# Router logits with the router's weights as the stationary operand, turned once per sequence

## What is computed

```
logits = x.astype(jnp.float32) @ gate_w.astype(jnp.float32).T        # (512, 256) @ (256, 8) for each sequence
scores = jax.nn.softmax(logits, axis=-1)
topk_w, topk_i = jax.lax.top_k(scores, K)                            # K = 2
topk_w = topk_w / (topk_w.sum(-1, keepdims=True) + 1e-20) * SCALE
...
return y + _swiglu_mlp(identity, sw_gate, sw_up, sw_down)            # the experts' sum, and the shared expert
```

## Time and profile before

| | |
|---|---|
| device time, median of 3 runs | 2029.63 us (2025.75 to 2030.84) |
| span of the profiled execution, first to last instruction | 1935.2 us |
| time around the span (median less span) | 94.4 us |
| TensorE busy / granted clock, mean | 1745.9 us (90%) / 0.959 |
| VectorE, ScalarE, GpSimd busy | 65%, 52%, 41% |

### The profile page before, as it was taken

The page is one execution under the profiler, slowest core; times in us unless marked ns, Lnnn a source line. Parts: engine busy times, 40 slices in busy tenths (PEclk is TensorE's granted clock), DMA queues, the critical chain, the costliest instruction groups (busy, mean ns, idle before and its releaser), DMA issues.

```text
span 1935.2 us, 41720 instructions
## 1 busy us (share of the span) xinstructions
PE 1745.9 (90%) x12978; PEld 1428.4 (74%) x12979; DVE 1265.4 (65%) x3121; ACT 997.8 (52%) x2314; POOL 792.4 (41%) x970
## 2 busy tenths in 40 slices
PE   0699999999999999988899995999999999999995
PEld 0466666666666666655788894999999999978884
DVE  3477788888888787876667766533333333367885
ACT  0366676767767666666433333444444444434553
POOL 2045555555555555555368774000000000067771
PEclk9889899999999888998799998999999999999997
DMA  2555556666555564562264533222222222247884
GB/s 46 87 83 84 100 90 109 111 111 107 104 105 104 101 107 90 95 115 91 67 204 162 172 129 127 63 73 73 73 73 71 72 73 73 76 153 184 223 203 75
DMA packets 175902, 205.94 MB, mean 106 GB/s; under 512 B 28209, under 2 KB 142450, under 8 KB 175762
## 3 DMA queue, kind: packets, MB, share of 16 engines
q1 hardware_dynamic: 153874, 161.66, 37.9%
q0 software_dynamic: 20736, 41.96, 8.3%
q10 hardware_dynamic: 1152, 0.52, 0.2%
HBM read 84.34 MB, written 68.81 MB: 79 GB/s over the span
## 4 chain that ended last, share of the span: by engine, by line
PE 70%; DVE 8%; ACT 6%; issue 5%; POOL 5%; DMA 2%; SPq 2%; ACTq 1%; POOLq 0%; DVEq 0%
PE bank L2295 5%; PE bank L1530 5%; PE bank L485 5%; PE bank L2296 4%; PE bank L487 4%; PE bank L2297 4%; PE bank L486 4%; PE bank L1585 4%; PE bank L1550 4%; PE bank L1532 3%; PE bank L1531 3%; ACT prob L1026 3%; PE bank L2316 3%; PE bank L2318 3%; PE bank L2317 3%
## 5 line engine op out<-in xcount | busy, mean ns | idle before, releaser
L2438 POOL DMA_INDIRECT f_y<-yg_scratch,index_all x128 | 129.8, 1014 | 552.8 <-DMA yg_scratch<-b_y 514.1
L897 POOL TENSOR_SCALAR_AFFINE_SELECT prob<-prob 128x512 f32<-128x512 f32 x256 | 163.4, 638 | 397.4 <-ACT prob L1026 397.3
L1026 ACT ACTIVATE prob<-bank 128x512 f32<-128x512 f32 (+1 forms) x512 | 249.1, 539 | 117.2 <-PE bank L1572 114.6
L2186 DVE TENSOR_TENSOR b_h<-b_h,bank 128x352 f32<-128x352 f32 x136 | 70.9, 521 | 291.7 <-ACT b_h L2134 291.7
L1305 DVE COPY_PREDICATED bank<-from_prev,bank 128x512 f32<-128x512 int32 x192 | 133.0, 693 | 107.5 <-PE bank L1550 103.7
L1308 DVE TENSOR_REDUCE row_max<-bank 128x4 f32<-128x512 f32 x256 | 177.3, 693 | 27.7 <-PE bank L1550 20.4
L2295 PE MATMUL bank<-wgu_h,bxT_h 128*128 x544 | 180.5, 332 | 0.7 <-DVE bxT_l L2181 0.3
L2296 PE MATMUL bank<-wgu_l,bxT_h 128*128 x544 | 176.9, 325 | 0.0
L2297 PE MATMUL bank<-wgu_h,bxT_l 128*128 x544 | 176.1, 324 | 0.0
L2134 ACT ACTIVATE b_h<-bank 128x352 f32<-128x352 f32 x136 | 63.2, 465 | 211.4 <-PE bank L2297 211.3
L1585 PE MATMUL bank<-prob,v_sb 128*32 128x256 f32 (+1 forms) x2048 | 164.1, 377 | 0.5 <-ACT pvT L1033 0.5
(11 more groups left out here) (338 smaller groups left out, 5104.0 us busy)
## 6 DMA issues: line engine op xcount, KB each, us to landing
bx<-xg_scratch SPq DMA_DIRECT2D x136, 128.0 KB, 2.1
yg_scratch<-b_y SPq DMA_DIRECT2D x136, 128.0 KB, 1.7
kS<-qk_h SPq DMA_DIRECT2D x128, 128.0 KB, 3.7
qS<-qk_h SPq DMA_DIRECT2D x128, 128.0 KB, 5.9
x_in<-in_L_attn_x_dram SPq DMA_DIRECT2D x16, 512.0 KB, 4.9
kS<-qk_l SPq DMA_DIRECT2D x64, 128.0 KB, 4.9
qS<-qk_l SPq DMA_DIRECT2D x64, 128.0 KB, 6.7
x_res<-in_L_attn_x_dram SPq DMA_DIRECT2D x16, 512.0 KB, 3.9
```

The source lines that it names most:

```text
L897: op = e.affine_select(out=own, in_=own, compare_op=ALU.is_gt, fill=0.0, base=0, pattern=[[0, HG], [1, P]], channel_multiplier=-1)
L1026: e.activation(prob[:, u % SLOTS, 2 * hp:2 * hp + 2, 0:w], src[:, :, 0:w], ACT.Exp, scale=SCALE).then_inc(keyed.frees[hp], 1)
```

## The change

`logits` swaps its operands: `wr`, padded with zeros to 32 columns, becomes the stationary operand, and the turned rows `rF` the moving one, 128 columns a matmul. The four row tiles go to four column tiles of the array (32 columns each) and to four groups of 32 partitions in PSUM. The logits then lie with experts along partitions. So ACT copies them to SBUF (`keep_logits`, into a piece of `wgu_l` that is not yet in use), TensorE turns the 128 x 128 block in one transposing matmul (`turn_logits`), and DVE reads that (`take_logits`). The turned block lies in `psum[3]`, a bank in which `gate_up` puts results for odd n; so `gate_up(M,1)` now waits for `lg_read`, the count of `take_logits` done. On DVE, `take_logits("b",M)` and `choose_first("b",M)` come after `hidden_low(m,5)`, and `take_logits("a",M)` right behind `choose_second("b",M)` rather than in the middle of step M. In step 0, `take_logits("a",0)` stays where it was and now waits for a turn on TensorE behind `gate_up(0,2)`.

```diff
...
         pos_f = sb("pos_f", [P, T, 2])
-        wr = sb("wr", [P, C, E])
+        wr = sb("wr", [P, (C - 1) * E + PAD])
         before = sb("before", [P, P])
...
         rF = arena[:, 2 * T * D:2 * T * D + C * S].rearrange("p (c s) -> p c s", c=C)
+        lg_kept = wgu_l[:, E * C - 1, 1, 0:P].bitcast(f32)
         items = {"a": rows_a, "b": rows_b}
...
             xh2_ready, copied_a = sem("xh2_ready"), sem("copied_a")
+            lg_turned, lg_read = sem("lg_turned"), sem("lg_read")
             pos_ready, member_ready = sem("pos_ready"), sem("member_ready")
...
                 reached(pe, *small.drained(m, name))
-                for t in range(T):
-                    for c in range(C):
-                        op = nc.tensor.matmul(small_bank(name, m)[:, t * E:(t + 1) * E], rF[:, c, t * P:(t + 1) * P], wr[:, c, :],
-                                      start=(c == 0), stop=(c == C - 1))
+                for c in range(C):
+                    for t in range(T):
+                        op = nc.tensor.matmul(small_bank(name, m)[t * PAD:(t + 1) * PAD, 0:P], wr[:, c * E:c * E + PAD],
+                                      rF[:, c, t * P:(t + 1) * P], start=(c == 0), stop=(c == C - 1), skip_group_check=True)
                 op.then_inc(small.full(name), 1)
+
+            def turned_bank(kind, m):
+
+                return SM[0][:, P:2 * P] if m == 0 else psum[3][:, 0:P] if kind == "b" else psum[3][:, P:2 * P]
+
+            def turn_logits(pe, kind, m):
+
+                if m >= HALF:
+                    return
+                pe.wait_ge(*small.read(m, f"lg{kind}"))
+                reached(pe, lg_read, item_of(kind, m))
+                nc.tensor.matmul(turned_bank(kind, m), lg_kept, ident[:, :],
+                                 start=True, stop=True, is_transpose=True).then_inc(lg_turned, 1)
+
+            def keep_logits(act, kind, m):
+
+                if m >= HALF:
+                    return
+                name = f"lg{kind}"
+                act.wait_ge(*small.filled(m, name))
+                reached(act, lg_turned, item_of(kind, m))
+                nc.scalar.activation(lg_kept, small_bank(name, m)[:, 0:P], ACT.Copy).then_inc(small.free(name), 1)
...
                     return
-                name = f"lg{kind}"
-                route.begin(item_of(kind, m))
-                dve.wait_ge(*small.filled(m, name))
-                nc.vector.tensor_copy(L, small_bank(name, m)[:, 0:T * E].rearrange("p (t x) -> p t x", t=T)).then_inc(small.free(name), 1)
+                dve.wait_ge(lg_turned, item_of(kind, m) + 1)
+                nc.vector.tensor_copy(L, turned_bank(kind, m).rearrange("p (t x) -> p t x", t=T)[:, :, 0:E]).then_inc(lg_read, 1)
...
                     return
-                dve.wait_ge(*small.read(m, f"lg{kind}"))
+                route.begin(item_of(kind, m))
+                dve.wait_ge(lg_read, item_of(kind, m) + 1)
                 largest(dve, L, m1, k1, oh1)
...
                 if n == 4:
+                    keep_logits(act, "b", m + 1)
                     rows_copy(act, "a", m + 1)
+                if n == FCS - 1:
+                    keep_logits(act, "a", m + 1)
...
                     sp.dma_start(full, src).then_inc(piece_in[0], 16)
+                sp.wait_ge(ffn_zeroed, 1)
                 with nc.allow_non_contiguous_dma(reason="the router's 2048 weights, once"):
                     for c in range(C):
-                        sp.dma_start(wr[:, c, :], gate_w[:, c * P:(c + 1) * P].rearrange("e p -> p e")).then_inc(router_in, 16)
+                        sp.dma_start(wr[:, c * E:(c + 1) * E], gate_w[:, c * P:(c + 1) * P].rearrange("e p -> p e")).then_inc(router_in, 16)
                 body(SEQS - 1, 1)
...
                     e.memset(before[:, :], 1.0).then_inc(ffn_zeroed, 1)
-                    pool_.wait_ge(ffn_zeroed, 1)
+                    pool_.wait_ge(ffn_zeroed, 2)
                     e.affine_select(out=before[:, :], in_=before[:, :], compare_op=ALU.is_gt, fill=0.0, base=0,
...
                             select(i, u)
+                        if at(i, SEQS - 1) and u == 0:
+                            e.memset(wr[:, :], 0.0).then_inc(ffn_zeroed, 1)
                         if u == 2 and live(before):
...
                             rows_copy(act, "b", 0)
+                            keep_logits(act, "b", 0)
                         if at(i, SEQS - 1) and 8 <= u < 8 + 2 * C:
...
                     first_chunk(act, 0, n)
+                    if n == 1:
+                        keep_logits(act, "a", 0)
                 normed(2, SEQS - 1, x_res, (0, 1))
...
                             turn_rows(pe, "a", 0)
+                            turn_logits(pe, "b", 0)
                         if u == 7 and live(nxt):
...
                         hi, lo = (w[:, k, :, :].rearrange("p k f -> p (k f)") for w in (wgu_h, wgu_l))
+                        if k == CHUNKS - 1:
+                            gp.wait_ge(lg_turned, 2 * HALF)
                         gp.wait_ge(stage_in, 32 * (k + 1))
...
                             place(dve, "b", m)
-                            take_logits(dve, "a", m)
                             hidden_low(dve, m, 1, h_f, h_h, h_l)
...
                         hidden(dve, m, 4, h_f)
-                        take_logits(dve, "b", m + 1)
                         hidden_low(dve, m, 4, h_f, h_h, h_l)
-                        choose_first(dve, "b", m + 1)
                         hidden(dve, m, 5, h_f)
...
                         hidden_low(dve, m, 5, h_f, h_h, h_l)
+                        take_logits(dve, "b", m + 1)
+                        choose_first(dve, "b", m + 1)
                         choose_second(dve, "b", m + 1)
+                        take_logits(dve, "a", m + 1)
                     expert_blocks()
...
                         if m > 0:
+                            pe.wait_ge(lg_read, 2 * m + 2)
                             gate_up(pe, m, 1, rT_h, rT_l)
...
                         gate_up(pe, m, 2, rT_h, rT_l)
+                        if m == 0:
+                            turn_logits(pe, "a", 0)
                         shared_down(pe, m, 0, h_h, h_l)
                         gate_up(pe, m, 3, rT_h, rT_l)
+                        if m == 0:
+                            pe.wait_ge(lg_read, 2)
                         turn_rows(pe, "b", m + 1)
...
                         gate_up(pe, m, 5, rT_h, rT_l)
+                        turn_logits(pe, "b", m + 1)
                         if m == HALF - 1:
...
                             gate_up(pe, m + 1, 0, rT_h, rT_l)
+                        turn_logits(pe, "a", m + 1)
                         shared_down(pe, m, 5, h_h, h_l)
```

## The result

The changed kernel takes 2046.91 us (median of 8 runs, 2039.21 to 2056.41); the kernel before, run beside it, takes 2030.24 us (8 runs, 2025.75 to 2037.24). The ratio is 1.008, with a 95% interval of 1.0057 to 1.0103: the change makes the kernel slower, by some 16 us, and the forecast of 2028.7 (2019 to 2039) missed it.

What follows compares the result with a forecast made beforehand. TensorE was taken to bound the routing pass, up to waits for other engines. Terms -1.0 (beginning), 0, +2.8, -1.0 and -1.7 (clock) sum to -0.9, from 2029.63 to 2028.7 us; range 2019 to 2039.

Steps and rivals of the forecast that it cites:

- The wait behind `logits("b",M)`: At each boundary, `turn_rows("a",M)` waits 1.13 us for `keep_logits` on ACT, paid from 1.2 gained: net 0.
- the span's distance of 94 us to the median: Whole kernel: 94.4 us between span 1935.2 and median 2029.63 lie around the span and were taken as unchanged.
- The term of 0.05 us for the semaphore: Ahead of `turn_rows` at boundary 4: 0.05 us from the end of ACT's copy to TensorE's start.
- The wait ahead of `gate_up(M,1)`: At each boundary TensorE waits for VectorE's chain, reaching `gate_up(M,1)` at t + 10.4 to 12.5: +2.8 us in all.
- GpSimd's splits: VectorE's chain ahead of `gate_up(M,1)`: weight splits stretch it, three of seven boundaries at +1.2 us, four at -0.2.
- TensorE's busy time: Seven boundaries: shorter `logits` less added transposes would give 14.7 us if nothing waited.
- the stall of `rows_low` behind `choose_first`: VectorE at the boundaries: `choose_first` no longer stands ahead of `rows_low`; one such stall counted as gone, -1.0 us.
- The beginning: Start of the routing pass: shorter `logits("a",0)` saves 2.2 us, of which 1.0 is kept; `logits("b",0)` gives nothing.
- The clock: Routing pass: one of three stretches at the lower clock taken as gone, -1.7 us.
- Rival 3: VectorE's chain meets GpSimd at nearly every boundary, 1.9 us each: slower, 2042 us; chance 0.15.

Runs made afterwards that it cites:

- e8: The changed kernel without the scatter's indirect DMAs (memsets instead, expert blocks load rows of `xn2`, rows not routed): 1997.71 us, ratio 0.9827 to before.
- e13: The changed kernel with the scatter's indirect DMAs replaced by plain ones of the same bytes, rows not routed: 1992.16 us, ratio 0.9862 to before.
- e1: The kernel before, no edit, profiled a second time: 2026.99 us, span 2025.2 us.
- the short execution: The first profiled execution of the kernel before, no edit, from which the prediction was made: span 1935.2 us.
- e14: The kernel before with the scatter's indirect DMAs replaced by plain ones of the same bytes, rows not routed: 2012.67 us, ratio 0.9968 to before.
- e12: The kernel before with plain DMAs of the same bytes for the scatter, the same kernel as e14, on another chip: 2025.85 us (one run).
- e7: The kernel before without the scatter's indirect DMAs (memsets instead, expert blocks load rows of `xn2`, rows not routed): 2007.0 us, ratio 0.9858 to before.
- e2: The changed kernel with `keep_logits("b")` ahead of `hidden_high(m,4)` on ScalarE: 2030.98 us, ratio 0.9998 to before.

## Why the prediction was wrong

**The step that failed** is the price of the handoffs in **The wait behind `logits("b",M)`**: "a wait of 1.13 us, paid from the 1.2 gained. Net 0 (-0.1 to +0.1) at each boundary". The place and the releaser were right, and the size is right where no update comes late (1.04 at five of seven boundaries in e8 and in e13). In the kernel as it runs, the wait is 1.04 to 6.04 us, 21.2 over seven boundaries where before has 7.6. I had taken ScalarE's start from one row of an execution in which no signal was late, and had taken the span's distance of 94 us to the median as something around the kernel. It was inside it. I had also named only the end of `shared_down(m,2)` for `hidden_high(m,4)` to wait for; at boundaries 4 to 7 of the changed kernel VectorE's `hidden(m,4)` comes last. The term of 0.05 us for the semaphore had no row behind it: in e8 0.14 us lie between the end of the copy (1085.24) and `turn_rows` (1085.38).

**The wait ahead of `gate_up(M,1)`** was forecast at t + 10.4 to 12.5, +2.8 us in all. It is at t + 13.4 to 15.0, 6.9 us more than in e1 in all and 19.4 more than in the short execution that the forecast started from, with some 8 us of shorter `logits` inside. The cause given, GpSimd's splits, is not the main one: with the splits there and no late update it is 10.1 at five of seven boundaries (e8, e13), and 10.9 to 12.6 at the other two. That the transpose of "a" holds up `shared_down(m,5)` was not in the forecast at all: its handoff was taken as free.

**The sum of what was seen**, after against before over the pass: +13.6 at `turn_rows`, +6.9 up to `gate_up(M,1)`, -7.3 in the rest, mostly "b"'s own `logits`: +13.2. The remaining part of the difference between the two spans lies ahead of the pass (first `logits` at 919.3 and 911.4) and behind it; whether it belongs to the change was not tested. Executions of one kernel differ there by 4.9 us (911.4 and 916.3 before) and by 6.1 (e14 921.9, e12 915.8). The two executions of one kernel in e12 and e14 differ by 11.0 us in the pass, so the split of the 13.2 is that of these two executions; the 16 us rest on the timed runs.

**What was right:** `logits` at 0.57 for 0.6; the copy at 0.26 for 0.28; the transposes at 0.03 to 0.13 for 0.1; TensorE's busy time down by 13.0 for 14.7. The Trainium skill (TensorEngine Tiling (Array Packing), Performance Considerations) would have had `logits` at 0.45, by an estimate from its 4 times; the measured gain of 1.79 to 0.57 is 3.1 times, not 4. Its warning that the copy out of PSUM may become the bottleneck points at the right place, since TensorE waits for L614 in each kernel with the change. But the copy itself is 0.26 us of a wait of 1.04 to 6.04; the rest is what stands ahead of it on ScalarE, and the signals. **What was only of the wrong size:** the stall of `rows_low` behind `choose_first`, -1.0 in the forecast, is 4.6 us in two waits in e1 and 7.6 in five in e14, so the gain of moving the choice was too low. **The beginning:** `logits("b",0)` gives nothing, as forecast, though for another reason. TensorE waits for GpSimd's `rem` (L1726, 6.2 us), and it starts 8.5 us after the first `logits` in both kernels (919.3 to 927.8 after, 911.4 to 919.9 before). **The clock** gave nothing in the kernel as it runs: 0.91 in both, -1.7 was forecast. Where no update is late it gave 8.5 us (e8 against e7, e13 against e14).

**Rival 3** gave the right side and nearly the number, 2042, by a mechanism that the runs speak against; that is luck. That the indirect DMAs turn the change's sign is shown (e13 with e14; e7 with e8 point the same way). That they do it through late signals rests on the late starts, which come and go with them (the short execution apart), and on the five waits of 1.04 us without them. Not separated from it is what else changes with them: GpSimd is busy for 156 us of the pass with the indirect DMAs, 106 with plain ones, 50 with none, and its splits move. How the 16 us split among the three handoffs is not settled: alone, the first shows 7 us more wait at its place and the second 5.3 us more at its own, each in one execution, and neither is clear of noise in the time, so they don't add up to what the three do together. The first is needed for the loss (e2). Why the short execution had no late updates, with the same 128 indirect DMAs, stays open. So does whether signals are late when nothing is recorded: a span and a granted clock stand beside every timed run of the experiments, records are missing in just the stretches with the late signals, and no run here leaves the recording out.

## What to carry to other kernels

Hold the span of a profiled execution against the timed runs first: if they differ by several per cent, that execution is not the kernel that is timed, and the price of a wait read from it may be far too low (here 1.13 us for 1.04 to 6.04). A change that makes one engine's work shorter by adding engine-to-engine handoffs on its path pays for each the signal's delay in the kernel as it runs, not the copy's length; count the handoffs, and try the form with the fewest (here half of the change, with its copy ahead of the long instruction, gained 0.4% where the whole lost 0.8%). Taking away a suspected wait and adding it to the other kernel are two different measurements, and only both together say whether the costs add.

## What the runs showed of the hardware

- While GpSimd's indirect DMAs of 128 rows were being issued, or up to 1.5 us behind, some semaphore updates of TensorE, VectorE and ScalarE came late, 2.0 to 2.3 us in the median in e1 and after and 5.02 us at the place shown, and the engine that waits started that much later. In the routing pass this went away with the indirect DMAs (e7, e8) and also with plain DMAs of the same bytes from the same queue (e12 to e14: no late update, no late start). Late updates also stand in the last pass, where GpSimd gathers by 128 more indirect DMAs, in every kernel here with the scatter or without (at least 23 to 40 of them). The exception is the short execution: all its indirect DMAs, and no late update in either pass.
- In the same stretches the trace has no record for some updates (170 of 778 instructions in the pass of e1 have none of their own, 0 of 778 in e7). An update matched to the next record there looks later than it was.
- The indirect form takes GpSimd 0.96 us for each DMA and 1.27 us from one to the next; the plain form takes 0.54 us.
- Four column tiles of 32 with 16 records of 128 moving columns take 0.57 us, as long as the 8 records of 256 columns in the earlier trace rows.
- Of eight stalls of TensorE of 1.75 to 1.81 us (e12, e14), six were followed within 3.2 us by 3.4 or 6.8 us at a granted clock of 0.50, two were not.
